# A macaron transformer layer in fp32: filler matmuls with constant weights, an earlier start-up order and a smaller first load on one core

## The reference, cut to what matters

```python
B, S, D = 8, 512, 128
def _L0_ffn_ref(x, ...):                  # HEADS 16, dh 8, EXPERTS 8, DFF 512
    xt = conv1d(transpose(x), conv_w, padding 1) ; x = transpose(xt) + conv_b      # width 3
    q, k, v = split(x @ wqkv.T + bqkv)                                            # 16 heads of 8
    attn = softmax(q k^T / sqrt(8)) ; ctx = attn v
    x = layernorm(x + ctx @ wo.T + bo, ln1_g, ln1_b)
    probs = softmax(x @ gate_w + gate_b)                                          # all 8 experts
    h = relu(einsum('bsd,edf->bsef', x, w1) + b1) ; y = einsum('bsef,efd->bsed', h, w2) + b2
    return layernorm(x + einsum('bse,bsed->bsd', probs, y), ln2_g, ln2_b)
x = x + 0.5 * _L0_ffn_ref(layernorm(x))
x = x + _L0_attn_ref(layernorm(x))        # cheap dilated self-attention: softmax inside segments
x = x + 0.5 * _L0_ffn_ref(layernorm(x))
```

## Time and profile before

| | us |
|---|---|
| median of 3 runs | 1567.61 |
| lowest and highest | 1564.55, 1571.96 |
| profiled execution, its own time | 1570.9 |
| its span | 1569.1 |
| PE, DVE, ACT, POOL busy | 1506.0, 1161.9, 1121.3, 1015.1 |

### The profile page before, as it was taken

One profiled execution on the slowest core, in us unless ns is written; L12 is line 12 of the kernel. 1 busy time (PEld: TensorE's weight loads), 2 busy tenths in 40 slices (PEclk: granted clock), 3 DMA queues, 4 the chain that ended last, 5 costly groups with the idle time before them and its releaser, 6 DMA issues.

```text
span 1569.1 us, 25935 instructions
## 1 busy us (share of the span) xinstructions
PE 1506.0 (96%) x8226; PEld 825.1 (53%) x8226; DVE 1161.9 (74%) x1834; ACT 1121.3 (71%) x1636; POOL 1015.1 (65%) x978
## 2 busy tenths in 40 slices
PE   3788999999999999999999999999999999999997
PEld 2223555555555555555555555555555555555476
DVE  2667677877778787788877778777777777767486
ACT  2365777777776777767777676777777777777776
POOL 3421567767687676867768687766767677666343
PEclk9977999999999999999999999999999999999999
DMA  6442315132332523325143331523333251521111
GB/s 146 114 122 76 92 48 136 45 105 72 85 93 49 135 56 80 91 55 129 42 115 70 88 84 48 148 49 99 89 84 98 52 133 42 132 59 36 41 43 33
DMA packets 75308, 130.04 MB, mean 83 GB/s; under 512 B 10613, under 2 KB 39206, under 8 KB 70566
## 3 DMA queue, kind: packets, MB, share of 16 engines
q1 hardware_dynamic: 73894, 124.19, 31.1%
q0 software_dynamic: 1280, 4.20, 1.1%
HBM read 97.42 MB, written 29.62 MB: 81 GB/s over the span
## 4 chain that ended last, share of the span: by engine, by line
PE 84%; DVE 8%; issue 3%; DMA 2%; ACT 1%; SPq 1%; POOL 1%; DVEq 0%; ACTq 0%; POOLq 0%
PE hid_y L997 16%; PE ctx_ps L1167 15%; PE hid_y L1001 13%; PE hid_y L998 13%; PE score L1035 11%; PE misc L997 3%; DVE negmax L865 3%; PE misc L998 2%; PE misc L1001 2%; PE score L1055 1%; PE misc L1109 1%; DMA f_xn<-in_L_attn_x 1%; DVE x1n L346 1%; PE score L997 1%; PE misc L1125 1%
## 5 line engine op out<-in xcount | busy, mean ns | idle before, releaser
L865 DVE TENSOR_REDUCE negmax<-score 128x2 f32<-128x1024 f32 x484 | 590.7, 1220 | 225.2 <-PE score L1035 225.1
L578 POOL TENSOR_TENSOR hidl<-hid,hidh 128x512 fp32r<-128x512 f32 x456 | 584.3, 1293 | 258.2 <-DVE hidh L822 142.5
L695 ACT ACTIVATE probs<-score 128x1024 f32<-128x1024 f32 x468 | 479.5, 1025 | 108.9 <-PE score L1055 108.7
L724 ACT ACTIVATE hid<-hid_y,cols 128x512 f32<-128x512 f32 x484 | 330.9, 684 | 162.1 <-PE hid_y L1001 156.0
L1167 PE MATMUL ctx_ps<-probs,V 128*18 128x512 f32 x2048 | 278.6, 617 | 3.4 <-DVE ctxT L872 3.4
L1055 PE MATMUL score<-Qp,Kp 32*128 32x512 f32 (+1 forms) x1024 | 269.9, 508 | 2.7 <-ACT probs L688 2.5
L1035 PE MATMUL score<-Kp,Qp 24*128 24x512 f32 x968 | 246.6, 503 | 15.6 <-DMA Kp<-k_parts_dram 9.2
L997 PE MATMUL hid_y<-x1h,w1h 128*128 128x512 f32 x484 | 236.1, 488 | 1.5 <-DVE negmax L865 1.3
L366 POOL TENSOR_TENSOR yacc<-yacc,gated 128x512 f32<-128x512 f32 x127 | 170.5, 1343 | 61.8 <-DVE gated L838 61.8
L721 ACT ACTIVATE hidh<-hid_y,cols 128x512 fp32r<-128x512 f32 x256 | 174.6, 682 | 33.9 <-PE hid_y L1001 31.5
L997 PE MATMUL hid_y<-hidh,w2h 128*128 128x512 f32 x484 | 195.7, 404 | 0.0
(11 more groups left out here) (189 smaller groups left out, 1815.8 us busy)
## 6 DMA issues: line engine op xcount, KB each, us to landing
gate_b<-gate_dram SPq DMA_DIRECT2D x128, 256.0 KB, 3.6
q_parts_dram<-q_parts SPq DMA_DIRECT2D x48, 256.0 KB, 3.0
k_parts_dram<-k_parts SPq DMA_DIRECT2D x48, 256.0 KB, 3.0
Qp<-q_parts_dram SPq DMA_DIRECT2D x64, 192.0 KB
Kp<-k_parts_dram SPq DMA_DIRECT2D x64, 192.0 KB
Qp<-q_parts_dram SPq DMA_DIRECT2D x32, 240.0 KB
Kp<-k_parts_dram SPq DMA_DIRECT2D x32, 240.0 KB
Qp<-q_parts_dram SPq DMA_DIRECT2D x32, 144.0 KB
```

Source lines behind the costliest of these rows:

```text
L578: pool.tensor_tensor(hidl[:, n % RING, :], hid[:, n % 2, :], hidh[:, n % RING, :].bitcast(F32), ALU.subtract).then_inc(s["h_lo"], 1)
L695: act.activation(probs[:, n % 2, 2 * j:2 * j + 2, :], score2[:], ACT.Exp, scale=SCALE)\
L724: act.activation(hid[:, n % 2, :], hid_bank(u, n), ACT.Relu, bias=col(n))\
L865: dve.tensor_reduce(negmax[:, g % 2, :, k % 8], banks_for_max(u.count(32, k))[:], AX.X, ALU.max, negate=True).then_inc(s["a_max"], 1)
```

## The change

It has four parts.

- **Filler matmuls.** `keep_busy` issues matmuls of the identity with itself into `hid_y`: 20 ahead of unit 0's first transpose, 5 behind the weight transposes, 5 ahead of the q projection. `keep_clock` issues matmuls of 384 columns with the constant convolution weights into the bank that the round's own maximum scores then overwrite: 12 in round 14, one in each even round from 16 to 54. Nothing reads any of them.
- **Start-up order.** The convolution starts on `xh` and the high weights, and uses `xl` last; that holds for all units. PE no longer waits for the low qkv weights and for wo ahead of the convolution. q and k of unit 0 go into two banks of `score2`, so k need not wait for q's readers. The projections start on `ch` and wait for `cl` only ahead of their last matmul. In unit 0 `cl` waits for `ch` and no longer for the copy `conv`, which comes after it.
- **Loads.** Unit 0's first chunk has 2 head pairs instead of 5, its second chunk 6 instead of 3, and the second chunk goes ahead of the loads for the probabilities. Unit 1's x is loaded ahead of all of these (`SECOND_LOAD_AT`).
- **Tables.** `AT` is read through the unit, and `wait_misc` looks its predecessor up in a list over all units. Neither moves an instruction.

```diff
+FIRST_CHUNKS = (((0, 2), (2, PAIRS)), ((0, 4), (4, PAIRS)))
+CLOCK_FILL = {k: 12 if k == 14 else 1 if k % 2 == 0 else 0 for k in range(14, 56)}
+SECOND_LOAD_AT = -27
+BUSY = (20, 5, 5)
...
+        def qk_bank(n, k):
+
+            return misc[:] if n else score2[:, k, :]
...
+        FIRST_LOADS_AT = {-19: (0, 0, 0), -16: (1, 0, 0), -7: (0, 0, 1), -6: (1, 0, 1),
+                          1: (0, 1, 0), 2: (1, 1, 0), 25: (0, 1, 1), 26: (1, 1, 1)}
...
-                pe.wait_ge(s["ld_wo"], 16 * HG)
-                pe.transpose(turned_wo, wo_raw, ident[:]).then_inc(s["set_turned"], 1)
-                pe.wait_ge(s["set_ql"], 1)
+                keep_busy(BUSY[1])
+                pe.wait_ge(s["set_cl"], 1)
...
+            def keep_clock(k):
+
+                for _ in range(CLOCK_FILL[k]):
+                    pe.matmul(banks_for_max(k)[:, 0, 0:3 * D], cwh[:, 0, :], cwh[:].rearrange("p j o -> p (j o)"),
+                              start=True, stop=True)
...
+            def keep_busy(times):
+
+                for _ in range(times):
+                    pe.matmul(hid_y[:, 0, 0:128], ident[:], ident[:], start=True, stop=True)
...
+                    wait(pe, s["f_xh"], u.count(1, 1))
+                    for j in range(3):
+                        pe.matmul(misc[:], cwh[:, j, :], xh[:, j:j + S], start=(j == 0), stop=False)
+                        pe.matmul(misc[:], cwl[:, j, :], xh[:, j:j + S], start=False, stop=False)
                     wait(pe, s["f_xl"], u.count(1, 1))
                     for j in range(3):
-                        last = three(misc[:], cwh[:, j, :], cwl[:, j, :], xh[:, j:j + S], xl[:, j:j + S],
-                                     start=(j == 0), stop=(j == 2))
+                        last = pe.matmul(misc[:], cwh[:, j, :], xl[:, j:j + S], start=False, stop=(j == 2))
...
                     ready_for_max(u.n, T // 2)
+                    if 32 * u.n + T // 2 in CLOCK_FILL:
+                        keep_clock(32 * u.n + T // 2)
```

241 lines of the change are left out of this document (127 added, 114 removed).

## The result

The changed kernel takes 1558.91 us (median of 20 runs, 1555.21 to 1562.3); the kernel before, run beside it on the same chip, 1568.57 (20 runs, 1559.44 to 1578.19). The ratio is 0.9941, with a 95% interval of 0.9925 to 0.9956: 9.7 us or 0.6% faster. The forecast was 1548.0. The new time lies inside the range (1539 to 1559) only by 0.1 us at its slow end, and the gain is less than half of the 21.0 that the sum gave.

What follows compares the result with a forecast made beforehand. PE, busy 1506.0 of 1569.1 us, was taken as the bound, with the whole answer in the first 160 us. Terms summed to 21.0 us saved, 1549.9 from the profiled execution or 1546.6 from the median; forecast 1548, range 1539 to 1559.

Steps and rivals of the forecast that it cites:

- first scores: Start-up: reordered convolution, fillers and smaller first chunk bring the first scores from 38.40 to 29.5, 8.9 us earlier.
- x wait at round 9: Between rounds 8 and 9: unit 1's x has long landed, only DVE's own work stays of 4.57 us; 3.4 earlier.
- 12 fillers: Between unit 1's transposes and round 14's scores: nothing hides the twelve 384-column fillers; 3.2 us later.
- clock, 14 to 24: Old stretch 61.4 to 74.0: fillers make PE dense, upper clock level from round 14 on; 3.9 us saved.
- stretch 84 to 101: Low-clock stretch 84.3 to 101.4: if fillers hold the clock, 5.3 less about 2.3, so 3.0 us saved.
- stretch 115 to 135: Low-clock stretch 115.0 to 135.5: if fillers hold the clock, 6.4 us, taken as 6.0 for DVE's share.
- single fillers: One filler in each second round after round 14: 20 at 0.05 us each, 1.0 us lost; bounds 0 and 11.
- I take 4.3: Start-up: smaller first Kp load takes 4.3 us from issue to first scores instead of 7.5, a gain of 3.2.
- less about 2.3: Stretch 84.3 to 101.4: 2.3 us off its 5.3, as PE reaches the DMA of maxima sooner only to wait longer.
- the filler doesn't hold the clock: Rival: clock rises at round 14 and falls again after some 10 to 20 us; 12 us gained, 1556; chance 0.27.
- stay at the lower level: Rival: start at low clock, first scores only 3.2 us earlier; 1552 with clock held, 1561 without; chance 0.13.
- The slower rival: Even rounds 16 to 54: filler's weight loads lie open, 0.55 to 0.93 us each; 11 us slower, 1579; chance 0.04.

Runs made afterwards that it cites:

- e6: Changed kernel with the fifth and later expert weight loads held until the first chunk of Qp and Kp has landed: 1556.46 us, ratio 0.994.
- e4: Changed kernel with the old first chunks (5 head pairs first) and their old load order: 1563.74 us, ratio 0.997.
- e8: Changed kernel with the DMA of maxima issued by ScalarE in a queue of its own instead of SyncE's: 1579.4 us, ratio 1.0077.
- e9: Changed kernel with unit 1's first Kp load issued behind the third group's DMA of maxima: 1553.16 us, ratio 0.9886.
- e11: Changed kernel with unit 1's last normalisation step on GpSimd two rounds earlier, ahead of one weight split and one load: 1557.48 us, ratio 0.991.
- e14: Changed kernel without the 12 fillers ahead of round 14, keeping the single ones of rounds 16 to 54: 1556.34 us, ratio 0.9927.
- e13: Changed kernel again, unedited, as a control: 1558.03 us, ratio 0.994.
- e16: e12 with the sixth instead of the fifth weight load held: 1550.36 us, ratio 0.9882.
- e17: e16 without the 12 fillers ahead of round 14, only single ones in rounds 14 to 54: 1547.29 us, ratio 0.9879.
- e1: Changed kernel without any filler in rounds 14 to 54, start fillers kept: 1562.74 us, ratio 0.9959.
- e15: e12 without any filler ahead of rounds 14 to 54: 1558.23 us, ratio 0.9941.
- e2: Changed kernel without the 30 fillers of the start: 1556.18 us, ratio 0.992.
- e10: Changed kernel with the 12 fillers ahead of round 14 but without the single ones of rounds 16 to 54: 1564.61 us, ratio 0.9951.
- e5: Changed kernel with the two constant-row DMAs (into Kp and Qp) issued by ScalarE instead of SyncE: 1560.02 us, ratio 0.9955.
- e18: Kernel before with only single fillers added, one ahead of each second round from 14 to 54: 1562.42 us, ratio 0.998.
- e12: Changed kernel with the edits of e2, e6, e9 and e11 together: 1551.3 us, ratio 0.987.
- e3: Changed kernel with unit 1's x loaded behind unit 0's Qp and Kp loads again: 1559.97 us, ratio 0.9947.

## Why the prediction came out as it did

The forecast's mechanisms were there in the main: the x wait went, with the single filler the second low stretch went, the filler itself stayed hidden, nothing happened behind round 56. Its sum failed, and by its own terms so (predicted and measured are us saved, a minus is a loss):

| term | predicted | measured | |
|---|---|---|---|
| first scores | +8.9 | +3.7 | 38.40 to 34.69 |
| x wait at round 9 | +3.4 | +2.1 | rounds 0 to 9 |
| 12 fillers | -3.2 | -3.7 | rounds 13 to 14 |
| clock, 14 to 24 | +3.9 | +4.3 | |
| stretch 84 to 101 | +3.0 | -0.2 | rounds 24 to 30 |
| stretch 115 to 135 | +6.0 | +6.1 | rounds 30 to 47; 5.5 of it in rounds 40 to 47 |
| single fillers | -1.0 | not to be separated | rounds 47 to 56 lost 0.4 |

**The step that failed: "I take 4.3" for the load, and the 2.9 us kept for k's writes.** The computation came sooner than worked out: the 20 start fillers took 6.1 us, the transposes of x began at 7.96 and lost nothing (9.2 was predicted), and `ch` came at 13.0 (14.4). None of this helped, because SyncE's issuing was the limit, and q's three writes took 3.62 us of it instead of 1.82: the last write went out at 23.3, predicted 21.6. Behind the writes it took 4.7 us to the load's issue instead of 2.9, and 6.7 to the scores instead of 4.3: together 4.2 of the 5.2 that are missing; the rest is the 1.7 us by which the writes were late, less the 0.7 that had been added for the uncertain clock. The prediction took the size of both from rows of before and didn't ask which other transfers the earlier start would set free. It let the weights' splits come 10.5 us sooner, so four weight loads of 256 KB went out ahead of the `Kp` load. e6 held them and its first scores came 4.6 earlier, most of the 5.2. The 4.3 lies between the 2.93 us that the small load needs without the weight loads (e6) and the 6.66 beside them. The small chunk itself is worth more than the 3.2 us set for it: without it (e4) the first scores come 5.4 later.

On the same place the Trainium skill (SBUF — State Buffer, on the cost of a transfer) was weighed, with 0.7 us saved by the smaller chunk. As an estimate by that page 192 KB take 2.5 us. The trace is near it for the load with the weights held (e6: 2.93 us from its issue to the first scores) and far from it for the load beside other traffic (6.66), and the chunk was worth 5.4 us there and not 0.7; the measurements decide.

**The second step that failed: the stretch 84 to 101, "less about 2.3".** The clock term there was right in that the low level shrank from 17.1 to 6.8 us, and wrong in that nothing came of it, 3.2 us less than forecast: the prediction had 2.3 us taken off for "PE comes there sooner only to wait longer", and the wait took all. DMA of maxima 6.99 us instead of 5.27, rounds 27 to 28 6.19 instead of 3.02. e8 rules out the queue, e9 names the load that stands in front and takes 3.5 us back at that place. With these two steps (5.2 and 3.2) and the x wait (1.3) 9.7 us are told, where the sum and the trace are 9.0 apart (21.0 and 12.0 at round 56); the other terms make up the difference.

**The x wait.** "Only DVE's own work stays" was right, but 3.4 of 4.57 us leave room for one reduction alone. Between rounds 8 and 9 (2.43 us in after) DVE also has unit 1's statistics to do, and they are the missing 1.3:

```profile
45.72 0.86 DVE L823 BATCH_NORM_STATS2 f_st<-f_xn 128x6 f32<-128x128 f32 x4
46.72 0.38 DVE L828 BATCH_NORM_AGGREGATE f_mv<-f_st 128x2 f32<-128x6 f32 x4
```

GpSimd's chain behind them moved as a whole, but with a weight split (1.24) and a load's issue (0.81) inside; e11 moved one step ahead of them and got 2.2 us between rounds 13 and 14, of which nothing was left at round 56.

**The 12 fillers.** Their cost was sized well (3.84 us, at the lower level throughout) and their purpose misjudged. The forecast had them make PE dense and so raise the clock. e14 has the rise at 57.7 without them. By the medians they cost 1.7 us in one set (e13, e14), and 3.1 between e16 and e17, of two sets; by the traces at round 56 1.9 and 2.4. The gain of rounds 14 to 24 belongs to the single ones, as far as it belongs to the fillers: e1, without any, rises only at 69.7, but e15, also without any, at 53.1. What decides the time of the rise stays open.

**Which reading of PEclk was right.** The forecast went by durations, against the printed 1.00 up to 74 us. In after and e1 the column has an event early enough and prints 0.50 for the same kind of rounds (57.00:69.80 above), and the 3.9 us taken from it came out as 4.3. The durations were right at the start too: a convolution matmul took 0.63 us without fillers ahead of it (before at 14.60, e2 at 11.47) and 0.39 behind them (after at 10.87). The Trainium skill (TensorE: Matmul & The Clock Gate, Part 1) has the throttled state as the default, and the traces agree in this with these 0.63 us.

**The rivals.** That the filler doesn't hold the clock is refuted for the second low stretch. Without single fillers the traces (before, e1, e10, e15) have two low stretches of 13.6 us or more between the rise and 135; with them e5 and e18 have one such, and the others only shorter falls of up to 10.2 us (e17 none). The start didn't stay at the lower level: the printed clock was 1.00 from 4.3 to 21.4. Yet the first scores were nearly as late as that rival had them (3.7 earlier, against 3.2), by a cause that it didn't name. The second chunk wasn't late. The slower rival had the single filler at 0.55 us or more; a pair of rounds takes 3.18 us with it (hid_y scores at 79.74 and 82.92), as without.

**The size of the clock terms.** In the traces the fillers are worth 7.4 us at round 56 (e1), in the medians 3.8 in one pair of sets and 6.9 to 7.9 in the other (e15 against e12 and e16). Without fillers the runs of a kernel mostly lie 13 to 19 us apart (before in five of its six sets, e1, e15; before in the set of e9 to e12 8.4), with them 2 to 10 (e3 apart, with 15.8), and the fastest single run of e1 (1553.46) is faster than any of after's. So they seem to take away the bad draws more than they speed up the good ones, and the profiled execution of before, at 1570.9, was one of its bad draws. A sum made from that one promises some 2 us too much against the median.

Open stay: what raises the clock; why it fell at 85.6 in e9, where the wait was gone, and for 17 us in e5, where TensorE was never idle; and how much of the fillers' worth in the medians is the chance of the draws.

## What to carry to other kernels

When a change makes a start-up earlier, list every transfer that waits for the engines it speeds up, and look whether one now overtakes the transfer that you need: here four weight loads did, and cost 4.6 us of the 8.9 expected. See too which engine issues the DMAs: if it is never idle in the start-up, an earlier computation gives nothing. A short DMA is late not only by its queue but by large packets already at the DMA engines, so it should be issued ahead of them, not elsewhere. One small constant matmul per pair of rounds, put where TensorE waits anyway, took away a low stretch of 20 us here and wasn't seen in the length of a pair of rounds, but it is no guarantee (e5, e18); a burst of them on the path should be tried without, and the spread of the runs read along with the median.
